# A decoder layer's cross-attention: value product with the probabilities as the stationary operand

## The reference, cut to what matters

```python
def feature_map(x): z = einsum('nshd,ed->nshe', x, fm_w) + fm_b; return concat([exp(z), exp(-z)], -1)   # 8 -> 16
v, k, q = (feature_map(t) for t in (values, keys, query))          # values = keys = context, query = layernorm(x)
scores  = einsum('nqhd,nkhd->nhqk', q, k) / sqrt(128)
attn    = softmax(scores, axis=-1)                                 # over 77 keys
out     = einsum('nhql,nlhd->nqhd', attn, v).reshape(N, S, 256)
x       = x + out @ fc_w.T + fc_b
```

## Time and profile before

| | |
|---|---|
| median of 3 executions | 703.36 us (699.74 to 706.22) |
| profiled execution, first to last instruction (the only time given of it) | 651.5 us |
| TensorE busy (matmuls / weight loads) | 465.1 us / 320.6 us |
| VectorE, ScalarE, POOL busy | 341.3, 258.7, 202.1 us |
| mean granted TensorE clock | 0.829 of full speed |

### The profile page before, as it was taken

One profiled execution on the slowest core, in us unless ns is written; L12 is line 12 of the kernel. 1 busy time (PEld: TensorE's weight loads), 2 busy tenths in 40 slices (PEclk: granted clock), 3 DMA queues, 4 the chain that ended last, 5 costly groups with the idle time before them and its releaser, 6 DMA issues.

```text
span 651.5 us, 12002 instructions
## 1 busy us (share of the span) xinstructions
PE 465.1 (71%) x3697; PEld 320.6 (49%) x3698; DVE 341.3 (52%) x969; ACT 258.7 (40%) x578; POOL 202.1 (31%) x271
## 2 busy tenths in 40 slices
PE   0576767665766128898898888895899999877720
PEld 0354544453433116566575666652356666665710
DVE  4547666532566924656556666647583333333322
ACT  0434444436886003434334444453653222333310
POOL 3123222163788500000000000002105760388850
PEclk9969686866888555959769989997989999889875
DMA  5820000000666997986679889000004110567727
GB/s 104 293 77 2 0 0 0 2 0 15 180 182 177 183 182 102 116 96 83 87 93 121 94 109 119 12 4 1 1 2 130 54 46 0 152 209 237 248 74 218
DMA packets 101544, 61.88 MB, mean 95 GB/s; under 512 B 33896, under 2 KB 99720, under 8 KB 101384
## 3 DMA queue, kind: packets, MB, share of 16 engines
q1 hardware_dynamic: 92040, 52.92, 42.6%
q0 software_dynamic: 2560, 5.31, 2.2%
q10 hardware_dynamic: 6912, 3.25, 2.1%
HBM read 40.34 MB, written 20.73 MB: 94 GB/s over the span
## 4 chain that ended last, share of the span: by engine, by line
PE 41%; DVE 17%; SPq 14%; ACT 9%; issue 8%; DMA 7%; POOL 2%; ACTq 1%; DVEq 0%; POOLq 0%
PE bank L706 5%; SPq L468 4%; PE bank L691 4%; PE bank L1177 4%; PE bank L1187 4%; PE bank L1188 4%; ACT prob L848 3%; SPq L1232 2%; PE bank L735 2%; PE bank L729 2%; DMA y_back<-routed 2%; PE bank L661 2%; PE bank L431 2%; PE bank L723 2%; PE bank L396 2%
## 5 line engine op out<-in xcount | busy, mean ns | idle before, releaser
L848 ACT ACTIVATE prob<-bank 77x512 f32<-77x512 f32 x128 | 73.7, 591 | 105.8 <-PE bank L691 105.4
L865 POOL COPY vcur<-vals 77x272 f32 (+1 forms) x32 | 13.1, 416 | 190.7 <-PE bank L706 190.7
L706 PE MATMUL bank<-prob,vcur 77*17 77x128 f32 x1024 | 58.7, 305 | 12.1 <-ACT prob L848 11.6
L661 PE MATMUL bank<-kst,qst 96*128 96x77 bf16 x512 | 41.8, 228 | 33.5 <-DMA kst<-kparts 24.1
L773 DVE TENSOR_REDUCE mx<-bank 128x5 f32<-128x385 f32 (+1 forms) x96 | 53.9, 580 | 22.1 <-PE bank L661 19.9
L691 PE MATMUL bank<-qst,kst 99*77 99x128 bf16 x512 | 58.7, 247 | 2.1 <-DMA qst<-mT 2.1
L820 DVE COPY avs_s<-bank 128x512 f32<-128x512 f32 x32 | 22.1, 691 | 57.9 <-PE bank L706 57.9
L691 PEld LDWEIGHTS bank<-qst,kst 99*77 99x77 bf16 x512 | 45.6, 135 | 11.3 <-issue 4.5
L661 PEld LDWEIGHTS bank<-kst,qst 96*128 96x128 bf16 x512 | 32.6, 117 | 37.0 <-DMA kst<-kparts 12.4
L1151 POOL DMA_INDIRECT routed<-t_y,t_no x48 | 47.2, 984 | 8.1 <-POOL carrier_p L1150 5.1
L936 DVE TENSOR_TENSOR act<-bank,s_g 128x512 f32<-128x512 f32 x32 | 22.0, 689 | 45.6 <-ACT s_g L1092 45.5
(11 more groups left out here) (167 smaller groups left out, 1000.2 us busy)
## 6 DMA issues: line engine op xcount, KB each, us to landing
qst<-qparts SPq DMA_DIRECT2D x96, 128.0 KB, 4.5
t_w<-in_expert_w SPq DMA_DIRECT2D x48, 192.0 KB
qparts<-qpart SPq DMA_DIRECT2D x16, 384.0 KB, 3.4
kparts<-kpart SPq DMA_DIRECT2D x48, 77.0 KB
kst<-kparts SPq DMA_DIRECT2D x16, 231.0 KB, 6.6
sorted_in<-fill SPq DMA_DIRECT2D x1, 3168.0 KB, 10.5
t_row<-sorted_in ACTq DMA_DIRECT2D x48, 66.0 KB
kst<-kparts SPq DMA_DIRECT2D x16, 154.0 KB, 6.9
```

Source lines behind the costliest of these rows:

```text
L661: i = pe.matmul(bank[n % 2][:, (h - h0) * KEYS:(h - h0 + 1) * KEYS], qst[r][0:ROWS, h, j * S:(j + 1) * S], kst[r][0:ROWS, h, j * KEYS:(j + ...
L706: i = pe.matmul(bank[4][32 * c:32 * c + EX + 1, (u - 1) * P:u * P], av_lhs(g, r, j, 4 * (u - 1) + c), prob[(u - 1) % 2][:, c], start=True, ...
L848: a.activation(prob[u % 2][:].rearrange("p c t -> p (c t)"), bank[2 + u % 2][0:KEYS], ACT.Exp, scale=SCORE_SCALE).then_inc(s["expd"], 1)
```

## The change

The operands of the value product change places: the probabilities of a head (77 keys by 128 queries) are the stationary operand, and the head's 77x17 values are streamed. The result has queries in rows at once, the 16 heads side by side in 272 columns of one bank, bank 4 and bank 6 in turn for the two sequences. So VectorE's copy to `avs` and the four transposes of t1 go. VectorE takes reciprocal and product straight from that bank, as soon as the sequence's last value product is done, in place of the copy; t2 and t3 stay at u = 2 and u = 4 of the next sequence. Where the semaphores of the removed steps had kept order, waits take their place: before the shift's transpose and before the output product into bank 5 (on the residual add, `x2`), and before the first value product of a sequence (on `avn` of the sequence before last).

```diff
@@ sb3 tiles
-        avs = sb3("avs_s", [P, 512])
+        BK_AV = (bank[4], bank[6])
@@ turn_shift
+                if not (isinstance(g, int) and g < 2):
+                    pe.wait_ge(s["x2"], (g - 1) * JA - 1)
                 pe.wait_ge(s["mlo"], g + 1)
@@ attend
-                    if u == 1 and tails:
-                        tails[0]()
                     if u > 0:
                         n = j * 4 + u - 1
                         pe.wait_ge(s["expd"], g * (4 * JA) + (n + 1))
                         if u == 1:
                             pe.wait_ge(s["v_cur"], g * JA + (j + 1))
-                        if u == 1 and not (is_first(g) and j == 0):
-                            pe.wait_ge(s["avs"], g * JA + j)
+                        if u == 1 and not is_first(g):
+                            pe.wait_ge(s["avn"], g * JA + (j - 1))
                         for c in range(4):
-                            i = pe.matmul(bank[4][32 * c:32 * c + EX + 1, (u - 1) * P:u * P],
-                                          av_lhs(g, r, j, 4 * (u - 1) + c), prob[(u - 1) % 2][:, c],
+                            h = 4 * (u - 1) + c
+                            i = pe.matmul(BK_AV[j][:, h * (EX + 1):(h + 1) * (EX + 1)],
+                                          prob[(u - 1) % 2][:, c], av_rhs(g, r, j, h),
                                           start=True, stop=True)
                         i.then_inc(s["avp"], 1)
                     if u == 2 and tails:
+                        tails[0]()
+                    if u == 4 and tails:
                         tails[1]()
-                    if u == 4 and tails:
-                        tails[2]()
...
-            def av_lhs(g, r, j, h):
+            def av_rhs(g, r, j, h):
                 return vcur[(r % 2) * JA + j][:, h]
@@ tail (TensorE)
-                def t1():
-                    pe.wait_ge(s["avs"], g * JA + (j + 1))
-                    for u in range(4):
-                        i = pe.transpose(bank[6][:, u * P:(u + 1) * P], avs[:, u * P:(u + 1) * P], ident[:])
-                    i.then_inc(s["tavp"], 1)
...
                 def t3():
                     pe.wait_ge(s["t2"], g * JA + (j + 1))
+                    if not (is_first(g) and j == 0):
+                        pe.wait_ge(s["x2"], g * JA + j)
...
-                return [t1, t2, t3]
+                return [t2, t3]
@@ tail (VectorE)
-                    v.wait_ge(s["tavp"], b + 1)
-                    av = bank[6][:].rearrange("p (h w) -> p h w", w=32)
+                    v.wait_ge(s["avp"], g * (4 * JA) + (4 * j + 4))
+                    av = BK_AV[j][:, 0:HEADS * (EX + 1)].rearrange("p (h w) -> p h w", w=EX + 1)
@@ body (VectorE)
                         maxima(g + 2, j * 3 + 1)
-                    if back:
-                        tail(*back, 1)
                     if more:
                         maxima(g + 2, j * 3 + 2)
-                    v.wait_ge(s["avp"], g * (4 * JA) + (4 * j + 4))
-                    v.tensor_copy(avs[:], bank[4][:]).then_inc(s["avs"], 1)
+                    tail(g, j, 1)
                     if back:
                         tail(*back, 2)
...
-            tail(NA - 1, 1, 1)
             tail(NA - 1, 1, 2)
```

More of the change, by code:

```diff
@@ L134, in decoder_layer @@
                   "qres", "qmid", "qlo", "ctxTp", "ctxT", "zkp", "kf", "khi", "kres", "kmid", "klo", "vp", "v_ready",
-                  "ap", "amax", "neg", "mhi", "mres", "mmid", "mlo", "mTp", "mT", "bp", "expd", "avp", "avs",
-                  "ones_rows", "set", "v_cur", "tavp", "rden", "avn", "t2p", "t2", "fcp", "x2", "stat3", "mean3",
+                  "ap", "amax", "neg", "mhi", "mres", "mmid", "mlo", "mTp", "mT", "bp", "expd", "avp",
+                  "ones_rows", "set", "v_cur", "rden", "avn", "t2p", "t2", "fcp", "x2", "stat3", "mean3",
                   "xb2", "std3", "xn3", "h_kept", "hTp", "hT", "lgp", "lgT", "lgtp", "lg", "r_step", "oh", "rankp",
```

## The result

The changed kernel takes **851.6 us** (median of four runs, 847.94 to 853.8), the kernel before 704.79 beside it (699.74 to 708.82): ratio 1.207, 95% interval 1.2004 to 1.2137. The forecast was 862 us, range 745 to 905. The profiled execution took 847.94 us and its span is 846.1 us, so 1.8 us lie around the span.

What follows compares the result with a forecast made beforehand. TensorE was taken to bound cross-attention after the change, through float32 loads at the low clock. 26 sequences +128.3, four without scores +22.8, first two +7.6, in all +159 on 703.4: 862 us, range 745 to 905.

Steps and rivals of the forecast that it cites:

- L735's end of the bounds: Value-product pass priced like L735's 128-column float32 load: 0.21 us at 1.2 GHz, against 0.067 for L661's bfloat16 record.
- The second rival: Cross-attention at the high clock throughout because back-to-back loads count as activity: 698 us, ends 691 to 706; chance 0.12.
- The argument from the earlier trace: In cross-attention, busy TensorE alone did not raise the clock; rises came after streams without value products, so 0.50 stays.
- 0.72 against 0.11: Chances: low clock in all of cross-attention, 850 to 895 us (0.72), against clock changing level, some 740 to 850 (0.11).
- What stays of a sequence: Low-clock cross-attention sequence without transposes and old value products: 8.00 - 1.02 - 2.43 = 4.55 us.
- the 26 sequences: Cross-attention sequences that also compute a later pair's scores: 11.27 us each at the low clock, +128.3 us in all.
- The chain almost all L706: Sign expected in the profile after: the chain of waits almost all the value product L706.
- The four sequences: Cross-attention sequences without scores of a later pair: 10.20 us each against 18.01 for all four, +22.8 us.
- the first two: First two cross-attention sequences, already at the low clock: 4.3 us dearer each, less 1.02 for the second's transposes, +7.6 us.
- Waits costed at nothing: New waits in cross-attention on the scaled result, residual add and value products: met earlier or covered, no cost.
- The 51.9 us around the span: Timed median 703.36 us of the kernel before over its traced span 651.5; left as it is and carried into the forecast.
- The high-clock sequence: Cross-attention sequence after the change at 2.4 GHz: 4.55/2 + 32 x 0.11, plus up to 0.4: 5.8 to 6.2 us.

Runs made afterwards that it cites:

- s128_rows128: Changed kernel with each value product streaming 128 columns instead of 17 and zero rows filling its operands from 77 to 128 rows: 710.87 us, ratio to before 1.0237.
- bf16_operands: Changed kernel with probabilities and values rounded to BF16, one pass per head instead of two: 684.09 us.
- half_loads: Changed kernel with one load serving two heads' values, 34 columns streamed, odd heads' own probabilities left out: 745.84 us, ratio to before 1.0743.
- s64_rows128: Changed kernel with 64 streamed columns instead of 17 and operands zero-padded from 77 to 128 rows: 853.33 us, ratio to before 1.2292.
- s128_rows77: Changed kernel with 128 streamed columns instead of 17, probabilities and values keeping 77 rows: 721.87 and 767.86 us in its two runs.

## Why the prediction was right, point by point

- **Price of a load.** 0.21 us per pass at the low clock, from L735's end of the bounds, measured 0.2135; the other end, L661's 0.067, would have been wrong by a factor of three. At the high clock 0.11 was taken, and neighbouring passes in s128_rows128 mostly start 0.112 us apart. "TensorE: Matmul & The Clock Gate" of the Trainium skill (LDWEIGHTS) has a formula, columns over 1.2; an estimate by it is 107 ns for 128 columns. The trace agrees at 2.4 GHz, and not at 1.2, where it is twice that. The same page of the Trainium skill (Weight-path perf modes) has faster loads for 128 columns that aren't FP32. The loads of bf16_operands agree, 111 ns each on average against 332, and 28.9 us busy for 512 of them, so that they overlap; no run here separates that mode from the halved number of passes and the changed clock.
- **Which clock.** The forecast held at its strongest and least certain point: 0.50 from the stage's first sequence to its last, with TensorE busy for 346.1 of 347.1 us. The second rival, loads keep the clock up, fell in the changed kernel itself; half_loads and s64_rows128 repeat it. The argument from the earlier trace rows, that streams and not occupation go ahead of a rise, stood the test of s128_rows128. But it was weaker than it read: stretches without value products did not suffice. The two sequences at 0.50 that it sets against the rise begin with such a stretch too. Below, for the value product alone (records, us busy, clock), stand that of the second one and the 3 us before the rise in s128_rows128:

```profile
284.40:287.40 3.00, 0.00 (x0) 0.00 (x0) 0.50 1.16 169
...
246.00:249.00 3.00, 2.45 (x12) 2.22 (x11) 0.50 1.32 145
```

The first has no value product, TensorE was busy in it throughout, and the clock stayed at 0.50 to 292.38; in the second the value product, streaming 128 columns, takes most of the time, and the clock rose. So the level was forecast rightly, but what decides it was not known. Nor was it as safe as 0.72 against 0.11 sounds: s128_rows77 shows that the same loop can leave the low level in mid-stage. None of the four runs of the changed kernel shows such a rise in its time (847.94 to 853.8).
- **What stays of a sequence.** 4.55 us were forecast beside the 32 passes; 11.06 - 6.83 = 4.23 were measured; with the passes (0.11 the other way) that is 26 x 0.21 = 5.4 us, the whole difference of the 26 sequences (+128.3 forecast, +122.9 measured). Most of the 0.32 stands in two steps of the timeline of before, ahead of the two value-product groups that begin at 322.23 and 323.83:

```profile
321.76 0.53 PE L661 MATMUL bank<-kst,qst 96*128 96x77 bf16 x5
...
323.27 0.63 PE L691 MATMUL bank<-qst,kst 99*77 99x128 bf16 x4
```

These took 0.47 and 0.56 us to the start of the next; now the same steps take 0.34 (445.34 to 445.68) and 0.42 (444.92 to 445.34). So 0.27 us that went with the old product lay ahead of its own first records, where the working counted them to the scores and left them in; what takes this time there is not shown.

- **A sign that was not met.** "The chain almost all L706": from 440 to 452 us the value product has 62.7% of the chain, the scores and the output product most of the rest. They are TensorE too, so the bound is the one forecast.
- **The small terms.** The four sequences +22.8, measured +23.7; the first two +7.6, measured +5.7; the tail, left out, -1.1. Sum +159, measured +151.2.
- **Waits costed at nothing.** Right: in the stage TensorE waits 1.0 us for the exponential and 0.5 us for `avnT` in all, none of the new waits shows, and ScalarE's later exponentials wait for TensorE, which is the bound.
- **The 51.9 us around the span.** The step "I leave this part as it is" gave the right total by luck. In every trace whose own time is known 1.8 or 1.9 us lie around the span, so the profiled execution of before was most likely a short one. Its stage 4 took 207.6 us (443.89 to 651.47), where the profile taken later has 261.8 and the changed kernel's 251.0.
- **The high-clock sequence.** 5.8 to 6.2 us were forecast for the second rival, and s128_rows128, the run that comes nearest to that rival (its passes stream 128 columns), has 6.60: 32 passes of 0.112 are 3.58, near the forecast, but 3.02 us stay instead of 2.28 to 2.7, among them up to 0.31 us of a first wait on the exponential. So in place of the rival's 698 us stands 710.87, and even at the full clock the change in float32 is no gain here. The 5.28 us taken for the kernel before at this clock were not typical either: the pair of sequences from 298.85 to 310.30, all at 1.00, took 6.17 and 5.28, and later pairs 6.17 and 4.98.

## What to carry to other kernels

Swapping the operands of a product exchanges streamed columns for loaded ones; in float32 a 128-column load is paid twice per product, and these loads set the pace here, with 17 streamed columns as with 64, so price them (here at 0.2135 us each) before counting the transposes that go. Price them at the clock which the new mix will get, not at that of now: a TensorE that was busy for 328 of 329 us, almost all of it with loads, stayed at 1.2 GHz. Where operands may be two bytes wide, the same swap can pay: here it did, with zero rows in both orders. And where a matmul uses fewer than 128 rows, zero rows are worth a try: they add no streamed column, and 17 to 23 us of the 26 sequences came back for them, by the two traces of the float32 kernel before.

## What the runs showed that was not expected

- More work can be less time: 7.5 times the streamed columns took 141 us off the changed kernel, and zero rows 22.6 us off 26 sequences of the kernel before, both with a higher granted clock. How much streaming is enough was not settled: 64 columns on 128 rows did nothing, with 128 on 77 the clock rose in mid-stage.
- Stage 4 is not touched by the change and still varies. In the changed kernel, ScalarE stands twice for 12.8 and 19.6 us at L1085 (start, duration, line, tiles, count, idle time before and what ended it):

```profile
670.18 0.60 ACT L1085 ACTIVATE s_g<-bank 128x512 f32<-128x512 f32 x1 [12.83 <-remote]
690.42 1.09 ACT L1085 ACTIVATE s_g<-bank 128x512 f32<-128x512 f32 x2 [19.64 <-remote]
```

In the second profile of before one such hole has 27.6 us, in the first there is none, and the later traces all have two of 9 to 26 us (some put down to "issue"), at the time when POOL issues its 32 indirect transfers (L1136 in the changed kernel). What ScalarE waits for there the trace does not show, and the cause stays open. The 651.5 us were no typical span: stage 4 is 54 us longer in the second profile.
